# Two cross-attention layers on one core: another cyclic order, other lags and other banks for the five engines

## What is computed

```
def layer0(h, ctx):
    q, k, v = h @ Wq.T, ctx @ Wk.T, ctx @ Wv.T              # per head
    out = softmax(q k^T / 4) v
    return out @ Wo.T + bo + h

def layer1(h, ctx, mask):
    text, ip = ctx[:, :-4], ctx[:, -4:]
    probs_t = softmax(q k_t^T / 4)
    text_out = probs_t @ v_t
    qsem = l2norm(probs_t @ text)                            # 512 wide
    fused = q k_ip^T / 4 + 0.5 * (qsem @ l2norm(ip)^T)
    ip_out = (softmax(fused) * mask) @ v_ip
    return (text_out + ip_out) @ W_out + b_out + h
```

## Time and profile before

| | |
|---|---|
| median of 3 runs | 2695.78 us |
| profiled execution: its time, its span | 2705.6 us, 2703.8 us |
| mean granted TensorE clock over the span | 0.975 |
| busy share of the span: PE, DVE, ACT, POOL | 89%, 59%, 61%, 64% |
| DMA | 316.77 MB, 117 GB/s |

### The profile page before, as it was taken

The page is one execution under the profiler, slowest core; times in us unless marked ns, Lnnn a source line. Parts: engine busy times, 40 slices in busy tenths (PEclk is TensorE's granted clock), DMA queues, the critical chain, the costliest instruction groups (busy, mean ns, idle before and its releaser), DMA issues.

```text
span 2703.8 us, 83514 instructions
## 1 busy us (share of the span) xinstructions
PE 2395.2 (89%) x32568; PEld 1480.4 (55%) x32568; DVE 1608.1 (59%) x2829; ACT 1659.9 (61%) x2522; POOL 1721.5 (64%) x1311
## 2 busy tenths in 40 slices
PE   7999948989898999989899899998999989899985
PEld 5677724555555555555555555555555555555542
DVE  4422224666666666666666666666666666666664
ACT  2212126767677776766677677776767667777762
POOL 3122035777776767777777677777767777777773
PEclk9999958999999999999999999999999999999997
DMA  8667512434334443334343444443434344344432
GB/s 279 208 214 221 186 51 72 111 97 110 102 106 108 109 109 105 102 99 108 105 107 105 109 109 111 110 109 105 109 102 110 100 109 107 103 111 110 109 89 59
DMA packets 324451, 316.77 MB, mean 117 GB/s; under 512 B 165616, under 2 KB 265840, under 8 KB 324080
## 3 DMA queue, kind: packets, MB, share of 16 engines
q1 hardware_dynamic: 324080, 311.65, 41.7%
HBM read 174.09 MB, written 112.27 MB: 106 GB/s over the span
## 4 chain that ended last, share of the span: by engine, by line
PE 32%; DMA 14%; DVE 11%; issue 10%; POOL 9%; ACT 9%; SPq 3%; DVEq 0%; ACTq 0%; POOLq 0%
PE psum L903 11%; PE psum L985 7%; POOL e L1306 7%; DVE wr L1160 5%; PE psum L967 5%; DMA keys<-k_dram 5%; DMA r_dram<-rd 4%; ACT ef L1087 4%; DVE mneg L1146 3%; PE psum L999 3%; ACT eh L1101 3%; PE psum L906 2%; DMA rb<-r_dram 2%; DVE ust L1223 2%; PE psum L1012 1%
## 5 line engine op out<-in xcount | busy, mean ns | idle before, releaser
L1306 POOL TENSOR_TENSOR e<-ef,eh 73x1024 f32<-73x1024 f32 x320 | 676.7, 2132 | 163.3 <-ACT eh L1101 163.3
L1087 ACT ACTIVATE ef<-psum 77x1024 f32<-77x1024 f32 (+1 forms) x640 | 617.0, 1020 | 144.7 <-PE psum L969 140.1
L1146 DVE TENSOR_REDUCE mneg<-psum 128x8 f16<-128x616 f32 (+1 forms) x640 | 465.5, 768 | 222.4 <-PE psum L935 194.5
L1160 DVE TENSOR_TENSOR wr<-psum,e 73x1024 f32<-73x1024 f32 x320 | 390.1, 1220 | 231.4 <-PE psum L999 180.0
L967 PE MATMUL psum<-q,keys 32*77 32x256 f32 (+2 forms) x6144 | 412.8, 362 | 36.9 <-DVE mneg L1146 31.1
L1274 POOL TENSOR_TENSOR al<-ust,ah 128x768 f16<-128x768 f32 x128 | 210.4, 1643 | 242.7 <-ACT ah L1123 228.4
L985 PE MATMUL psum<-ef,values 128*32 128x256 f32 x5120 | 346.5, 388 | 17.0 <-ACT ef L1087 15.5
L999 PE MATMUL psum<-eh,gram 128*73 128x512 f16 x1280 | 328.8, 388 | 5.8 <-ACT ef L1087 5.8
L1101 ACT ACTIVATE eh<-ef 73x1024 f16<-73x1024 f32 x320 | 331.0, 1054 | 1.6
L1094 ACT ACTIVATE ust<-psum 128x512 f32<-128x512 f32 x384 | 224.1, 595 | 85.5 <-PE psum L985 85.0
L1269 POOL TENSOR_TENSOR ust<-ust,rb 128x768 f32<-128x768 f32 x128 | 231.5, 1808 | 69.0 <-DMA rb<-r_dram 68.9
(11 more groups left out here) (157 smaller groups left out, 4226.3 us busy)
## 6 DMA issues: line engine op xcount, KB each, us to landing
rb<-r_dram SPq DMA_DIRECT2D x128, 384.0 KB
keys<-k_dram SPq DMA_DIRECT2D x128, 231.0 KB, 3.9
values<-v_dram SPq DMA_DIRECT2D x128, 192.5 KB
x<-in_x SPq DMA_DIRECT2D x64, 384.0 KB, 4.0
ust<-ust SPq DMA_DIRECT2D x512, 48.0 KB, 2.1
v_dram<-vst SPq DMA_DIRECT2D x16, 1280.0 KB
out<-outt SPq DMA_DIRECT2D x64, 320.0 KB, 2.9
k_dram<-kst SPq DMA_DIRECT2D x32, 616.0 KB, 4.6
```

The lines of the kernel that those rows point to most:

```text
L1087: act.activation(ef[l][0:m, unit_heads(n), :].rearrange("t h s -> t (h s)"), src, ACT.Exp).then_inc(s_exp[l], 1)
L1146: dve.tensor_reduce(dst, o, AX_X, ALU.max, negate=True).then_inc(s_max[l], 1)
L1160: dve.tensor_tensor(wr[0:m, k % LOW_RING, :, :].rearrange("t (r h) s -> t r (h s)", r=2), banks(l, f"u{k}", 2)[0:m, :, :], e2[0:m, k % LOW ...
L1306: pool.tensor_tensor(e2[0:m, k % LOW_RING, :, :], ef[1][0:m, unit_heads(k), :], eh[0:m, unit_heads(k), :], ALU.subtract).then_inc(s_e2, 1)
```

## The change

Nothing that is computed changes, and no function. The tables `ORDER` and `USES` get other contents: each engine has the same steps in another cyclic order, with other lags (largest lag 6, before 5), and the 8 banks have other sequences of uses. The PE list of both, and one bank:

```
-        0t0/1 1s2/3 1m/3 0t1/1 1t0/3 0a0/1 1o/5 0o/2 0t2/1 0a1/1 1i/3 1t1/3 0q/0 1u0/3 1t2/3 0a2/1 1a0/3
-        0s0/0 1u1/3 1u2/3 1q/2 0s1/0 1a1/3 0s2/0 1n0/3 1a2/3 1u3/3 1p/4 1n1/3 1u4/3 1n2/3 1s0/2 1n3/3 0m/0
-        1n4/3 1s1/2""",
+        0o/3 0t0/1 1u2/4 1a1/4 0t1/1 1q/3 0t2/1 0a0/1 1a2/4 1s0/3 0a1/1 1s1/3 1n0/4 0a2/1 1n1/4 1s2/3 1u3/4
+        1m/3 1u4/4 1n2/4 1t0/3 0q/0 1t1/3 1p/5 1n3/4 1n4/4 0s0/0 1i/3 0s1/0 1u0/3 1t2/3 1a0/3 0s2/0 1o/5
+        1u1/3 0m/0""",
...
-    "0t0/1 0t3/1 1o/5 0t4/1 1t2/3 1u0/3 0s1/0 1q/2 1n/3",
+    "1y/5 1n/4 0s3/0",
```

More of the change, by code:

```diff
@@ L114 @@
     "pe": """
-        0t0/1 1s2/3 1m/3 0t1/1 1t0/3 0a0/1 1o/5 0o/2 0t2/1 0a1/1 1i/3 1t1/3 0q/0 1u0/3 1t2/3 0a2/1 1a0/3
-        0s0/0 1u1/3 1u2/3 1q/2 0s1/0 1a1/3 0s2/0 1n0/3 1a2/3 1u3/3 1p/4 1n1/3 1u4/3 1n2/3 1s0/2 1n3/3 0m/0
-        1n4/3 1s1/2""",
+        0o/3 0t0/1 1u2/4 1a1/4 0t1/1 1q/3 0t2/1 0a0/1 1a2/4 1s0/3 0a1/1 1s1/3 1n0/4 0a2/1 1n1/4 1s2/3 1u3/4
+        1m/3 1u4/4 1n2/4 1t0/3 0q/0 1t1/3 1p/5 1n3/4 1n4/4 0s0/0 1i/3 0s1/0 1u0/3 1t2/3 1a0/3 0s2/0 1o/5
+        1u1/3 0m/0""",
     "act": """
-        0m/1 1n/4 0t0/1 0t1/1 1m/3 0g/2 0t2/1 0t3/1 1t0/3 1t1/3 1h0/3 0a0/1 1r/3 1h1/3 0t4/1 0a1/1 1i/3 1f/4
-        1t2/3 1t3/3 0q/0 1h2/3 1t4/3 0a2/1 1a0/3 1h3/3 1h4/3 1q/2 1a1/3 0r/0 1a2/3 1g/4""",
+        0m/1 1r/4 0t0/1 0t1/1 0r/1 0t2/1 0t3/1 1f/5 1a1/4 1q/3 0t4/1 0a0/1 1a2/4 1h4/4 0a1/1 0a2/1 1m/3
+        1t0/3 1t1/3 0q/0 1h0/3 1t2/3 1t3/3 1n/4 1i/3 0g/2 1g/5 1h1/3 1t4/3 1a0/3 1h2/3 1h3/3""",
     "dve": """
-        1s1/3 1s2/3 1s3/3 1s4/3 1d/4 1y0/4 1y1/4 1y2/4 1y3/4 1y4/4 1y5/4 1y6/4 1o/5 1y7/4 1y8/4 1y9/4 1y10/4
-        1y11/4 1y12/4 0o/2 1y13/4 1y14/4 1y15/4 1y16/4 1y17/4 1y18/4 1y19/4 1y20/4 1w0/3 0s0/0 0s1/0 1w1/3
-        1w2/3 0s2/0 0d/1 0s3/0 0s4/0 1w3/3 1p/4 1w4/3 1s0/2""",
+        1y0/5 1y1/5 1d/5 1y2/5 1y3/5 1y4/5 1o/6 1y5/5 1w1/4 1y6/5 1y7/5 1y8/5 0o/3 1y9/5 1y10/5 1y11/5
+        1y12/5 1w2/4 1y13/5 1y14/5 1y15/5 1y16/5 1y17/5 1y18/5 1y19/5 1y20/5 1s0/3 1s1/3 1s2/3 1s3/3 1s4/3
+        1w3/4 1w4/4 1p/5 0s0/0 0s1/0 0s2/0 0s3/0 0d/1 1w0/3 0s4/0""",
     "pool": """
-        0at/2 0al/2 1vb/4 1b0/3 0xh/0 0xl/0 1kb/2 1xh/2 1xl/2 1c/3 0kd/0 0qh/0 1b1/3 1b2/3 1at/4 1b3/3 1b4/3
-        1kd/2 1qh/2 1al/4""",
+        1b2/4 1xh/3 1kd/3 1xl/3 1vb/5 1b3/4 1qh/3 1at/5 1b4/4 0kd/0 0xh/0 0xl/0 0at/2 0qh/0 1c/3 1b0/3 1kb/2
+        1al/5 0al/2 1b1/3""",
     "sp": """
-        1g/3 1ns/4 0v/1 1d/4 1nl/4 1vi/4 1sh/4 0x/0 1v/3 1sl/4 1st/5 1rw/4 1rl/4 0k/0 1ps/4 1ss/3 1k/2 1pl/4
-        0ds/1 0d/1 0sh/1 0rw/1 0rl/1 1ds/3 1c/2""",
+        1sl/5 1k/3 1st/6 1rw/5 1ss/4 1rl/5 1vi/5 0k/0 0x/0 1ps/5 0rw/2 1ds/4 0rl/2 0v/0 1pl/5 1c/3 1g/3 1v/3
+        0ds/1 1d/4 1sh/4 0d/1 1ns/4 1nl/4 0sh/1""",
 }
 USES = [
[8 rows of a table removed]
[8 rows of a table added]
 ]
```

## The result

The changed kernel takes 2716.14 us in the median of 6 runs (2713.2 to 2732.94), beside 2696.94 us of the kernel before (2691.58 to 2703.88): a ratio of 1.0079, interval 1.005 to 1.0107. It is 0.8% slower, where 4.5% faster was forecast.

A forecast was written before the change was run, and what follows sets the result against it. PE was taken as the bound: 31.3 us of its own work plus losses 1.1, 0.3, 0.3, 0.2 and 0.1 for late DMAs gave 33.3 us a pass; with the ends, 2575 us, 4.5% faster, range 2530 to 2635 us.

The forecast's parts named there:

- The waits that go: PE's waits before `1m`, `0s0`, `0s1` and `0a0` were to go, as other steps or orders cover them.
- The shapes and PE's own work: PE's own 31.4 us a pass stays, but for one change of shape fewer, -0.1 us: 31.3 us.
- (a): From `0s0` to `1o`: DVE's path to `1w0` takes 5.03 us against PE's 3.95, loss 1.1 us a pass.
- (b): From `0t0` to `0t1`: the second exponential's bank takes 3.56 us against PE's 3.24, loss 0.3 us a pass.
- (c): From `0t2` to `0q`: keys' load, rounding and splits take 9.5 us against PE's 9.1; loss taken as 0.3 us.
- (d): From `1p` to `0s0`: DVE's sum of `1p` takes 1.82 us against PE's 1.64, loss 0.2 us a pass.
- a second path as long over ACT: In the stretch `0s0` to `1o`, a path through `1t2` and its exponential comes out about as long as DVE's.
- The step that failed: Allowance of 0.1 us a pass for late DMAs, taking 33.2 to 33.3 us, 2.0 us less than before.
- The prediction's last sentence: Wrong if POOL L1264 waits over 1 us for keys in most passes, or SP is late with keys or spread inverses.
- The keys are late: Rival: `0q` waits for keys rounded ahead of its input; landing at 7 us gives 34.1 us, 2625 us; chance 0.18.
- The one for slower, with 0.05: Rival: keys landing beyond 7.6 us make every pass longer; at 8 us 35.8 us, some 2725 us; chance 0.05.
- The ends: One more pass from largest lag 6: start -14 us, end +16 us, together +2 us on the span.

The follow-up runs named there:

- the second run: Kernel after, with store and spread of layer 0's inverses moved ahead of the keys' load in the DMA queue's list: 2609.9 us, 0.9682 of before.
- the short maxima: Kernel with spread, input load and rounded keys all moved, whose first four layer 0 maxima read 38 of 77 scores: 2598.25 us, 0.96 of before.
- The first run: Kernel after, with the load of `pt` moved ahead of the spread of layer 0's inverses and its values' load: 2747.94 us, 1.0212 of before.
- both moves: Kernel after, inverses' store and spread ahead of input and keys, input's load before keys', rounded keys behind the split: 2598.23 us, fastest leaving nothing out.

## Why the prediction was wrong

**The waits that go.** Right. The 1.03 us before `1m` are gone from the timeline, `0s0` no longer waits for POOL at all (before, in about half of the passes), `0a0` waits for nothing.

**The shapes and PE's own work.** Right in sum: PE is busy 32.16 us a pass before, 32.28 after and 31.75 in the second run, over whole passes from `0t0` to `0t0`. The -0.1 us of one shape change was tested by no run of its own.

**(a) to (d).** Their sum was right. The kernels in which `pt` is on time take 33.26, 33.18 and 33.32 us a pass, where 33.3 was forecast. So were the four stretches one by one. Their ends in one pass of the second run, from PE's timeline (`0t0`, `0t1`, `0t2`, `0q`, then `0s0` and `1o`; `1p` at 1745.93 stands above):

```profile
1725.86 0.67 PE L967 MATMUL psum<-q,keys 32*77 32x256 f32 x8
...
1729.27 0.67 PE L967 MATMUL psum<-q,keys 32*77 32x256 f32 x8
...
1732.94 0.46 PE L967 MATMUL psum<-q,keys 32*77 32x128 f32 x8
...
1742.38 0.60 PE L903 MATMUL psum<-xh,wq 128*128 128x256 f16 x4
...
1747.72 0.32 PE L935 MATMUL psum<-keys,q 32*128 32x154 f16 x8 [0.19 <-ACT ef L1087]
...
1752.67 0.61 PE L903 MATMUL psum<-ah,wo 128*128 128x256 f16 x4
```

(a) takes 4.95 us, (b) 3.41, (c) 9.44 and (d) 1.79, where the longer side of each sum had 5.03, 3.56, 9.5 and 1.82. What fills them is in part another thing than forecast. In (c) PE doesn't wait for the split input (3.4 us in 60 passes): its own 15 steps take 9.4 us, not 9.1, and the keys, taken with 5.50 us, land in 2.8 us in the median after:

```profile
keys<-k_dram SPq DMA_DIRECT2D x128, 231.0 KB, 2.8
```

At the end of (d), `0s0` waits for ACT (59 times, 11.0 us in all) and not for DVE's sum. And (a), given to DVE, has a second path as long over ACT, as the prediction said; the short maxima showed it. So that (c) and (d) came out is in part luck.

**The step that failed: "With 0.1 us for DMAs that land late, ... I take 33.3 us".** It measured 1.8 us (35.07 - 33.26). PE stands idle 2.79 us a pass after and 1.52 in the second run, which is 1.3 of it; the other 0.5 is longer busy time, of which some 0.2 go with the lower granted clock behind the waits (an estimate: 0.26 us a pass after, 0.06 in the second run), and 0.3 weren't separated. I had costed the compute lists of the new order and one load, the keys, and for all other transfers had let the durations of the order before stand; the list of the DMA queue, 25 steps, had got another order, and it had no part in the sum. The load of `pt` was not named. The durations before held for a queue in which four stores, two small loads and more stood behind the spread of layer 0's inverses. In the new list the load of `pt` follows it with only the values' load between, and all of it comes behind a hold of 6.2 us. The first run (a transfer ahead of the spread is on time, and the spread then late), the second (the spread elsewhere, both on time) and the one with a third of its bytes show this together. The prediction's last sentence did name the sign, that SP is "late with the keys or the spread inverses": POOL waits 2.0 us for the spread in every pass after. Its sum gave that no time.

**The rivals.** "The keys are late" had the right kind, a transfer that a compute step waits for, and the wrong transfer: POOL L1264 waits for its keys in no pass after (before, 126.9 us in 57 passes). The keys' load does matter, but by what it holds up: waiting for `0t2` at the head of the queue, it delays everything behind it. The one for slower, with 0.05, was the same mechanism at the keys; its chance was that of one load, when the list has fifteen.

**The ends.** Forecast +2 us against the old shape; measured, by the same formula, 2712.7 - (424.2 + 61 x 35.07 + 125.2) = +24 us. Two parts: "pass 2 is again one of layer 0 alone (23)" and pass 1 took 28.3 and 32.0 us from `0t0` to `0t0` (370.57, 398.86, 430.90; the second holds a `0o`, some 3 us), I think because the keys' load for the next batch waits for `0t2` and POOL rounds these keys ahead of the input. With layer 0's keys and input moved alone they take 24.3 and 30.7 us (366.71, 391.01, 421.70), which bears that out for 5.3 us of it. With both moves they take 24.3 and 27.2; why the spread's move gives 3.5 us more there wasn't tried. The granted clock is low in these passes in all kernels (from 395 to 410 us 0.65 before, 0.50 after, 0.73 with both moves), and its part wasn't separated. And the tail is 150.1 us from `0t0` of pass 64, against some 138 forecast (141 from the start of the pass, which begins with `0o`); that stayed at 148 in the best kernel, and what lengthens it wasn't tried.

Together: 61 x (35.07 - 33.3) = 108 us of passes and 22 us of ends are the 130 us by which the forecast span (2582.7) was missed. The ends alone would have left the time inside the range.

## What to carry to other kernels

When lists are reordered by lags and slots, the DMA queue is an engine with a list of its own: place each of its waits and look at what is issued just ahead of each load that an engine waits for (here, in the 6 us ahead). In this kernel a large transfer belonged into the stretch in which the queue would stand still, and a load that has to wait for a compute step behind those that needn't. And a DMA's duration from the old order is a duration behind its old neighbours: the keys' load went from 3.9 to 2.8 us in the median, while `1p` could start only 8.2 us after the issue of its own, in the pass shown. A late load can cost TensorE twice, by the wait and by the lower clock that was granted behind some of the waits.

## What the runs showed that was not expected

A 96 KB load (`pt`) was there only 8.2 us after its issue behind a 384 KB spread with a broadcast source, and there within 5.9 us without it; with a third of the spread's bytes it was there within 6.3 us. The spread itself, issued 1.5 us behind `pt`, was ready for POOL only 6.3 us after its issue (1506.37 to 1512.65). The mean DMA share of 0.40 over the even stretch told nothing of this: within one pass it ran from 0.06 (1727 to 1730 us) to 0.90 (1730 to 1733 us).

Moving one load of 384 KB, the input's, from 0.4 us behind the keys' load to 3.2 us ahead of it changed the pass by 0.6 us (35.07 to 34.47) though no engine waits for that load in the even passes: it acts through other transfers.
